# Reordering four engine queues and moving the causal mask of the transposed scores from TensorE to GpSimd, in an attention and two-expert block on one core

## The reference

```python
h = layernorm(x) * (1 + ca) + sa
q = h @ w_dq.T @ w_uq.T;  k, v = split(h @ w_dkv.T @ w_ukv.T)       # 16 heads of 16
attn = softmax(mask_causal(q k^T * SCALE)) v
x = x + ga * (attn @ w_out.T)
h = layernorm(x) * (1 + cb) + sb
top = argmax(h @ Wg.T)                                               # two experts
out0 = gelu(h @ W0a.T + b0a) @ W0b.T + b0b
out1 = relu(h @ W1a.T + b1a) @ W1b.T + b1b
x = x + gb * where(top == 0, out0, out1)
```

## Time and profile before

| | us |
|---|---|
| median of 3 runs | 622.9 (622.04 to 628.52) |
| profiled execution, its own time | 623.6 |
| its span, first to last instruction | 621.8 |
| TensorE matmul busy | 518.4 (83%) |
| TensorE weight load busy | 456.4 (73%) |
| VectorE busy | 461.5 (74%) |
| ScalarE busy | 390.9 (63%) |
| GpSimd busy | 305.9 (49%) |
| mean granted TensorE clock | 0.943 |

### The profile page before, as it was taken

The page is one execution under the profiler, slowest core; times in us unless marked ns, Lnnn a source line. Parts: engine busy times, 40 slices in busy tenths (PEclk is TensorE's granted clock), DMA queues, the critical chain, the costliest instruction groups (busy, mean ns, idle before and its releaser), DMA issues.

```text
span 621.8 us, 14267 instructions
## 1 busy us (share of the span) xinstructions
PE 518.4 (83%) x4912; PEld 456.4 (73%) x4912; DVE 461.5 (74%) x884; ACT 390.9 (63%) x585; POOL 305.9 (49%) x300
## 2 busy tenths in 40 slices
PE   5634667899898979989898989799898998989974
PEld 4423455688787969787877878697778897878773
DVE  3438172689898987888887889877788888785373
ACT  2424454767777767676776767676667776676521
POOL 6235232355565554556454555555464564552352
PEclk9957595999999998999998999999899999999998
DMA  8644363433425170706253352608062524201100
GB/s 267 154 54 73 47 82 60 75 65 58 100 46 110 30 127 1 145 9 101 53 77 77 51 103 37 116 0 150 4 94 63 76 62 77 63 1 37 35 17 18
DMA packets 43802, 43.74 MB, mean 70 GB/s; under 512 B 5344, under 2 KB 40800, under 8 KB 43760
## 3 DMA queue, kind: packets, MB, share of 16 engines
q1 hardware_dynamic: 43760, 43.19, 37.3%
HBM read 13.39 MB, written 4.23 MB: 28 GB/s over the span
## 4 chain that ended last, share of the span: by engine, by line
PE 62%; DMA 10%; issue 9%; SPq 8%; ACT 6%; DVE 4%; POOL 0%; ACTq 0%; POOLq 0%; DVEq 0%
DMA ks<-parts_k 7%; PE ps_s L382 7%; PE ps_t L402 6%; PE ps_t L419 5%; SPq L282 4%; PE ps_c L333 4%; PE ps_t L406 4%; PE ps_c L335 4%; PE ps_c L334 4%; PE ps_o L333 3%; PE ps_o L334 3%; PE ps_a L333 3%; PE ps_o L335 3%; PE ps_a L334 3%; PE ps_a L335 3%
## 5 line engine op out<-in xcount | busy, mean ns | idle before, releaser
L1248 POOL TENSOR_SCALAR_AFFINE_SELECT score_rows<-score_rows 128x512 f32<-128x512 f32 (+1 forms) x96 | 83.3, 869 | 135.6 <-ACT score_rows L792 135.6
L792 ACT ACTIVATE score_rows<-ps_s 128x1024 f32<-128x1024 f32 x96 | 98.6, 1027 | 75.5 <-PE ps_s L382 69.1
L944 DVE TENSOR_REDUCE mx<-score_rows 128x4 f32<-128x1024 f32 (+1 forms) x96 | 115.4, 1212 | 18.4 <-POOL score_rows L1248 18.4
L816 ACT ACTIVATE p<-ps_t 128x1024 f32<-128x1024 f32 x96 | 98.6, 1027 | 15.7 <-PE ps_t L406 15.0
L382 PE MATMUL ps_s<-ks,qs 96*128 96x256 bf16 (+1 forms) x512 | 63.1, 260 | 43.7 <-DMA ks<-parts_k 29.4
L382 PEld LDWEIGHTS ps_s<-ks,qs 96*128 96x128 bf16 x512 | 38.3, 103 | 55.9 <-issue 44.2
L402 PE MATMUL ps_t<-qs,ks 99*128 99x256 bf16 (+1 forms) x512 | 61.8, 255 | 10.2 <-DMA qs<-mx_rows 9.7
L1182 POOL TENSOR_TENSOR xs<-z,xs 128x512 f32<-128x512 f32 (+1 forms) x16 | 25.0, 1562 | 66.0 <-DVE z L1033 66.0
L1090 DVE CAST hid_hi<-hid 128x512 fp32r<-128x512 f32 x64 | 34.9, 545 | 24.4 <-ACT hid L782 23.3
L402 PEld LDWEIGHTS ps_t<-qs,ks 99*128 99x128 bf16 x512 | 39.5, 101 | 15.9 <-issue 6.3
L1236 POOL TENSOR_TENSOR hid_lo<-hid,hid_hi 128x512 fp32r<-128x512 f32 x32 | 42.9, 1354 | 7.9 <-DVE hid_hi L1090 7.9
(11 more groups left out here) (165 smaller groups left out, 1666.4 us busy)
## 6 DMA issues: line engine op xcount, KB each, us to landing
qs<-parts_q SPq DMA_DIRECT2D x96, 128.0 KB, 4.3
ks<-parts_k SPq DMA_DIRECT2D x96, 128.0 KB, 5.0
xs<-x SPq DMA_DIRECT2D x16, 256.0 KB, 4.8
gates<-gates_scratch SPq DMA_DIRECT2D x16, 256.0 KB, 4.1
out<-xs SPq DMA_DIRECT2D x16, 256.0 KB, 4.2
p<-wmod SPq DMA_DIRECT2D x1, 1024.0 KB, 6.2
p<-waT SPq DMA_DIRECT2D x1, 1024.0 KB, 8.4
p<-wmod SPq DMA_DIRECT2D x1, 512.0 KB, 5.4
```

What stands on the lines that cost most here:

```text
L792: act.activation(score_rows[c % 2][:], ps_s[:], ACT.Copy).then_inc(scores_out, 1)
L816: act.activation((p0, p1)[tile][:, h0:h0 + n, :], ps_t[:].rearrange("p (h s) -> p h s", h=n), ACT.Exp, scale=SCALE).then_inc(exp_done, 1)
L944: dve.tensor_reduce(dst, score_rows[c % 2][:].rearrange("p (h k) -> p h k", h=n), AX_X, ALU.max).then_inc(max_done, 1)
L1248: pool.affine_select(out=diag, in_=diag, compare_op=ALU.is_ge, fill=NEG, base=0, pattern=[[0, n], [-1, P]], channel_multiplier=1).then_inc ...
```

## The change

TensorE no longer adds the triangle: the twelve matmuls of line 406 per batch go, each score matmul of `st_chunk` starts and stops its own accumulation, and the constant `past_b` is not built. In its place GpSimd gets `hide`, six instructions per batch that write zero over the exponentials above the diagonal, each behind the exponential of its chunk; `values` waits for the sixth of them (`hidden`) where it waited for the sixth exponential.

Four lists change their order. SP issues the second and third parts of k in front of `load_maxima` and `load_gates`, and `load_gates` waits for `scaled` (the end of `gate_ffn`) where it waited for `out_ready` (the end of `add_ffn`). ScalarE runs `gelu(.., 0)` at the end of the step, ahead of `values_copy`, where it ran it as the first stage of the next step. VectorE runs `k_rest` and `k_second` ahead of `row_max(at(2), 5)` and `split_maxima`. GpSimd runs `q_third` and `k_third` right behind the last `hide_scores`, then `leave_to_split`, and only then `gate_ffn`, `hidden_low(at(3), 0)` and `add_ffn`.

```diff
--- before.py
+++ after.py
@@ -259,7 +257,7 @@
                     sp.wait_ge(clamp_ready, 4)
                     sp.dma_start(gates_dram, clamped).then_inc(gates_stored, 16)
                     sp.wait_ge(gates_stored, 16)
-                wait(sp, out_ready, b.n - 1)
+                wait(sp, scaled, b.n - 1)
                 sp.dma_start(gates[b.parity][:].rearrange("p g d -> p (g d)"), gates_dram[bass.ds(b.n, 1), :].to_broadcast([P, 2 * D])
                              ).then_inc(gates_in[b.parity], 16)
 
@@ -315,12 +313,12 @@
                 stack_q(at(0), 1)
                 stack_k(at(0), 0)
                 stack_q(at(0), 2)
+                stack_k(at(0), 1)
+                stack_k(at(0), 2)
                 load_maxima(at(1))
                 load_gates(at(2))
-                stack_k(at(0), 1)
                 store(at(4))
                 prefetch_x(at(-2))
-                stack_k(at(0), 2)
 
             pipeline(sp, step)
             for n in range(2):
@@ -397,13 +395,9 @@
                 wait(pe, exp_done, CH * b.n + c)
                 tile, h0, n = ST[c]
                 width = S - P * tile
-                a_bank = 512 // width
                 for h in range(n):
-                    pe.matmul(ps_t[:, h * width:(h + 1) * width], ks[b.parity][0:RM, h0 + h, tile * P:(tile + 1) * P],
-                              qs[b.parity][0:RM, h0 + h, tile * P:S], start=h % a_bank == 0, stop=False)
-                for bank in range(2):
-                    diag = ps_t[:, bank * 512:(bank + 1) * 512].rearrange("p (h q) -> p h q", h=a_bank)[:, :, 0:P]
-                    mm = pe.matmul(diag, ident_b[:], past_b[:].unsqueeze(1).to_broadcast([P, a_bank, P]), start=False, stop=True)
+                    mm = pe.matmul(ps_t[:, h * width:(h + 1) * width], ks[b.parity][0:RM, h0 + h, tile * P:(tile + 1) * P],
+                                   qs[b.parity][0:RM, h0 + h, tile * P:S], start=True, stop=True)
                 mm.then_inc(st_done, 1)
 
             def values(b):
@@ -411,7 +405,7 @@
                 if b.off:
                     return
                 pe.wait_ge(v_ready, b.n + 1)
-                pe.wait_ge(exp_done, CH * (b.n + 1))
+                pe.wait_ge(hidden, CH * (b.n + 1))
                 for g in range(4):
                     for n in range(4):
                         h = 4 * g + n
@@ -816,7 +810,6 @@
                 act.activation((p0, p1)[tile][:, h0:h0 + n, :], ps_t[:].rearrange("p (h s) -> p h s", h=n), ACT.Exp, scale=SCALE).then_inc(exp_done, 1)
 
             def step(at):
-                gelu(at(4), 0)
                 maxima_rows(at(2))
                 gelu(at(4), 1)
                 relu(at(4), 2)
@@ -842,6 +835,7 @@
                 exponentials(at(2), 5)
                 scores_copy(at(1), 5)
                 k_first(at(0))
+                gelu(at(3), 0)
                 values_copy(at(2), 0)
                 values_copy(at(2), 1)
                 rest_of_weights(at(0))
@@ -1109,11 +1103,11 @@
                 q_second(at(1))
                 rest_of_modulation(at(1))
                 row_max(at(2), 4)
+                k_rest(at(1))
+                k_second(at(1))
                 row_max(at(2), 5)
                 split_maxima(at(2))
-                k_rest(at(1))
                 hidden_high(at(4), 0)
-                k_second(at(1))
                 late_low_part(at(1), 4)
                 divide(at(3), 0)
                 hidden_high(at(4), 1)
@@ -1155,13 +1149,6 @@
                                pattern=[[-1, P]], channel_multiplier=1).then_inc(consts_ready, 1)
             pool.wait_ge(consts_ready, 2)
             pool.tensor_copy(ident_b[:], ident[:]).then_inc(consts_ready, 1)
-            pool.memset(past, 0.0).then_inc(consts_ready, 1)
-            pool.wait_ge(consts_ready, 4)
-            pool.affine_select(out=past, in_=past, compare_op=ALU.is_ge, fill=NEG, base=0,
-                               pattern=[[1, P]], channel_multiplier=-1).then_inc(consts_ready, 1)
-            pool.wait_ge(consts_ready, 5)
-            pool.tensor_copy(past_b[:], past).then_inc(consts_ready, 1)
-
             def inverse_deviation(b, n):
 
                 if b.off:
@@ -1248,6 +1235,17 @@
                 pool.affine_select(out=diag, in_=diag, compare_op=ALU.is_ge, fill=NEG, base=0,
                                    pattern=[[0, n], [-1, P]], channel_multiplier=1).then_inc(scores_hidden, 1)
 
+            def hide(b, c):
+
+                if b.off:
+                    return
+                tile, h0, n = ST[c]
+                pool.wait_ge(exp_done, CH * b.n + c + 1)
+                wait_alone(pool)
+                diag = (p0, p1)[tile][:, h0:h0 + n, 0:P]
+                pool.affine_select(out=diag, in_=diag, compare_op=ALU.is_ge, fill=0.0, base=0,
+                                   pattern=[[0, n], [1, P]], channel_multiplier=-1).then_inc(hidden, 1)
+
             pool.wait_ge(blank, 1)
             inverse_deviation(Batch(0, 0, NB), 0)
 
@@ -1265,21 +1263,27 @@
                 hidden_low(at(4), 1)
                 first_inverse(at(0))
                 add_attn(at(3))
+                hide(at(2), 0)
                 hide_scores(at(1), 0)
                 inverse_deviation(at(3), 1)
+                hide(at(2), 1)
                 hide_scores(at(1), 1)
                 h_low(at(0))
+                hide(at(2), 2)
                 hide_scores(at(1), 2)
+                hide(at(2), 3)
                 hide_scores(at(1), 3)
                 g_low(at(3))
+                hide(at(2), 4)
                 hide_scores(at(1), 4)
+                hide(at(2), 5)
                 hide_scores(at(1), 5)
+                q_third(at(0))
+                k_third(at(0))
+                leave_to_split(at(1))
                 gate_ffn(at(4))
+                hidden_low(at(3), 0)
                 add_ffn(at(4))
-                q_third(at(0))
-                leave_to_split(at(1))
-                k_third(at(0))
-                hidden_low(at(3), 0)
 
             pipeline(pool, step)
 
```

More of the change, by code:

```diff
@@ L105, in block_kernel @@
         ident_b = sb("ident_b", [P, P], BF16)
-        past_b = sb("past_b", [P, P], BF16)
         neg_half = sb("neg_half", [P, TT])
@@ L161, in block_kernel @@
         cT_raw, c_silu = mx[:], mx_rest[:]
-        past = y[:, 0, 0:P]
         clamped, sign = [g[:].rearrange("p g d -> p (g d)")[0:NB] for g in gates]
@@ L181, in block_kernel @@
             "s_done scores_out scores_hidden max_done max_split mt_done".split())
-        mt_ready, st_done, exp_done, pv_done, o_ready = (sem(n) for n in "mt_ready st_done exp_done pv_done o_ready".split())
+        mt_ready, st_done, exp_done, hidden, pv_done, o_ready = (sem(n) for n in "mt_ready st_done exp_done hidden pv_done o_ready".split())
         ot_done, rden_ready, attn_ready, at_done, a_hi_ready, a_lo_ready, op_done, gated_ready, x1_ready = (sem(n) for n in
@@ L602, in _ @@
             mm.then_inc(wq_done, 1)
-            pe.wait_ge(consts_ready, 6)
+            pe.wait_ge(consts_ready, 3)
             pe.wait_ge(blank, 3)
```

## The result

The changed kernel takes 642.2 us in the median (637.6 to 642.7) against 623.7 for the kernel before on the same chip: a ratio of 1.027, 95% interval 1.019 to 1.034. The forecast was 600 and faster. Of the 19 us between the two profiled executions' spans 14 come from the twelve full steps, 4 from the filling, 1 to 2 from the emptying.

A forecast was written before the change was run, and what follows sets the result against it. Bound: the vector section (15.84 us) plus the rest of the round (17.31), 33.15 us a step. Forecast step 31.8 us; 16 us off twelve full steps, 5 emptying, 2 filling, together 23 off 623.6: 600 us, range 570 to 618.

The forecast's parts named there:

- Nothing for both: SP's list: moving `load_maxima` behind three more DMAs and `load_gates` ahead of the store and x's load costs nothing.
- `mx_rows` late because k's data is ahead of it in the DMA engines: Sign, for the profile after, that the forecast is wrong: the maxima's rows held up by k's data; no size given.
- GpSimd's contention: Rival: GpSimd's selects add 2.4 us to the vector section, full steps stay as they were; 616 us, chance 0.10.
- starvation: Rival: back-to-back GpSimd selects hold VectorE's seven port-using operations; section from about 18.3 us, at 20 us 644 us; chance 0.12.
- section: VectorE's stretch from `hidden_high(at(4), 3)` to the end of `ckv_low`: 15.84 us before, forecast 15.84 - 0.54 + 1.05 = 16.35.
- the clock: Rival: without the wait for k's DMA, TensorE's half clock goes in four of twelve steps, 2 us each; 592 us, chance 0.12.
- about as long: Argument against the clock rival: TensorE will wait at `expand_k` about as long as it did for k's DMA.
- k's stacking is worth nothing in the round: First score chunk: its 1.67 us wait for k's last DMA lies beside the vector section, so removing it alone gains nothing.
- Both old waits: TensorE's waits of 1.33 us at `turn_maxima` for the first gelu and 1.67 us at the first score chunk for k; both go.
- the rest: Rest of the round, `expand_k` to the next `hidden_high(at(4), 3)`: 17.31 us before, forecast 15.45 after gelu, first triangle and `relu`.
- The filling and emptying: Pipeline ends outside the twelve full steps: 2 us won while filling, 5 us while emptying.
- the 1.05: Vector section: us added by GpSimd's selects, one full hold-up of 1.00 plus a little waiting of `row_max` for `hide_scores`.

The follow-up runs named there:

- the maxima first: Changed kernel with the maxima's DMA issued ahead of k's second and third parts, these still ahead of the gates: 611.9 us, ratio 0.986 to the kernel before.
- ScalarE's queue: Changed kernel with the maxima's DMA issued by ScalarE and the gates' load behind the store on SP: 631.2 us, ratio 1.018 to the kernel before.
- work in the wait: Changed kernel with 14 matmuls, whose result nobody reads, in front of `expand_k`: 647.0 us, ratio 1.040 to the kernel before.
- triangle back: Changed kernel with the triangle on TensorE again and no selects of the exponentials on GpSimd, k still ahead of the maxima: 636.6 us, ratio 1.020.
- all three runs of the table: Changed kernel (642.2 us); it with the maxima on ScalarE's queue and gates behind the store (631.2 us); it with half of k's second and third stacking data (630.7 us).

## Why the prediction was wrong

Put in a row, each step with its ratio to the kernel before: k ahead of the gates 0.974; gelu sooner as well 0.952; the new order on VectorE and GpSimd, with q's and k's third parts sooner, and the gates' wait for `scaled` 0.944; the selects in place of the triangle 0.986; k ahead of the maxima too, which is the change, 1.027. The order of the row is chosen, and the parts don't add: the first three are worth 35 us by the ratios, the mask costs 26, and the place of one DMA another 26.

**The step that failed** is the sentence on SP, "`load_maxima` now stands behind three more DMAs, but these have gone out before the maxima are turned, so it isn't later in a full step", and its "Nothing for both". Issued it is not later; it lands later. I had counted SP's time and not that of the data: with k's 384 KB freshly issued in front, `st_chunk` could start only 5.5 to 6.7 us after the end of k's last issue, 6.5 to 6.7 in seven of the twelve full steps. The maxima's first packet moved 2.2 us after their issue where it had been 1.4, and their last increment came 4.7 us after it where it had been 2.8. I had named it as something that would make the prediction wrong ("`mx_rows` late because k's data is ahead of it in the DMA engines") and given it neither a price nor a chance. My rivals for a slower kernel were GpSimd's contention and starvation; the 644 us of the latter match the result by chance, for its mechanism (a section of 20 us) did not occur.

Why it costs 2 us a step and not 1.2: it closes a round of its own. k's parts can be made only after `expand_k`, which follows `ckv_low`; then come the issues, the landing of the maxima, `st_chunk`, and the next vector section. From the end of `ckv_low` to `st_chunk` it is 13.7 us in the changed kernel (328.91 to 342.59), where with the maxima first it is 11.0 at full clock and 12.5 behind a fall. The 13.7 hardly depend on the clock: with ScalarE's queue and the clock up it is 13.5, TensorE is there 1 us sooner and waits 2.10 us. So a fall between `expand_k` and `values` is nearly free inside this round, and "work in the wait" and "triangle back" bought next to nothing until the maxima went first. A fall behind the wait for the maxima isn't free: the step of the changed kernel from 365.83 us on has one and takes 36.6 us.

**The clock** is the second step. The rival "the clock" gained where TensorE's long waits were taken away; in the forecast itself I held that TensorE would wait at `expand_k` "about as long" and left the number of falls at four. In the changed kernel a fall follows the wait of 1.5 us there in ten of twelve full steps. With the maxima first, filling it ends the falls and brings the step from 32.6 to mostly 31.8 us. With the wait at 0.47 us there was no fall. The Trainium skill, TensorE: Matmul & The Clock Gate, § HAM oscillation, was right in kind: waits between bursts of matmuls throttle. Its first case is a wait for DMA; here it was a wait for VectorE. But the same 1.5 us are followed by a fall in only six of twelve steps with the maxima first, and in one of twelve in the run with the gates behind the store. The wait takes part, then, and doesn't decide alone; what else does stays open.

**That k's stacking is worth nothing in the round** was wrong too. I had called the section independent of TensorE's wait because the wait ended after it began. Alone it is worth 16 to 18 us: the section held 1.06 us that were TensorE's lateness in disguise, and the falls of the clock, which cost four steps 2 us each, came behind that wait and were gone without it.

**What was right.** Both old waits went. A full step is section plus rest, and without the maxima's DMA and with the clock up the rest is 15.4 (15.45 forecast). The filling and emptying, forecast 7 us shorter, came 5 us longer. The selects take about what `hide_scores`' rows said, though the larger is held up more often:

```profile
L1246 POOL TENSOR_SCALAR_AFFINE_SELECT p<-p 128x512 f32<-128x512 f32 x64 | 42.2, 660 | 6.2 <-ACT p L810 6.2
L1246 POOL TENSOR_SCALAR_AFFINE_SELECT p<-p 128x1024 f32<-128x1024 f32 x32 | 41.3, 1291 | 10.6 <-ACT p L810 10.6
```

`values` waited for them only twice. The section's 16.35 was hit by luck, by two errors that cancel: it starts from 14.78, not 15.30, and the selects add 1.58, not 1.05. The reason given for the 1.05 was a misreading too: four row maxima of 1.21 us are 4.8 us, under a third of the section and not most of it. `leave_to_split` did its work: the cast in the split takes 0.18 us in every step, where its median was 1.15.

**What stays open.** Halving k's data took 0.5 us off the maxima's way, less than half of what k's data seems to cost. The rest lies in how long the maxima's packets and the increments behind them take. In all three runs of the table that wait for the maxima, packets of other DMAs moved beside theirs; whether these are the cause wasn't tried. Nor was any run made that tells what besides a wait makes the clock fall.

## What to carry to other kernels

Cost a moved DMA by when it lands, not by when it is issued: list what data is in flight in front of it, in any queue, and put small urgent transfers ahead of large ones that can wait. Before calling a wait hidden beside another engine's chain, ask how much of that chain's length is itself waiting or contention caused by the same lateness; one edit alone on the kernel before would have shown it. And work moved from the busiest engine to an idle one is dear if its instructions lengthen those of the engine that really closes the round: 1.58 us on 14.78 here.

## What the hardware showed

- A small DMA (24 KB) behind 384 KB of stacking DMAs let its reader start 6.6 us after the last of these was issued, and 6.4 us from a queue of another engine; without them 3.4 us from its own issue sufficed. From the other queue its first packet moved 3.5 us after its issue, against 1.4 in the kernel before. The Trainium skill, DMA: Bandwidth & Descriptors, § Queues, rings and completion order, has the rule that a DMA's semaphore increment lands only after every earlier write of the same DMA engine, across its queues. The traces agree with it as far as they go, but leave it little: from the last packet to the last increment are 1.1 to 1.3 us, against 0.9 before. Most of the delay is in the data itself.
- In the changed kernel TensorE's clock fell to its lower level behind waits of 1.5 us in ten of twelve full steps; in two other runs the same waits were followed by a fall in six and in one of twelve. It stayed at the higher level through 31-us steps with waits of 0.5 us. Matmuls that compute nothing, put into the wait, kept it up and made the kernel 7 to 8 us faster, but only once no DMA closed the round.
- Six selects on GpSimd, 5.2 us of its time, lengthened a VectorE list of 14.78 us by 1.58 us, though GpSimd had that time free. A `tensor_scalar` of 128x2 in this list took 1.04 us where it took 0.17 without them.
